# Cross attention and a feed-forward stack on one core: shifting scores in four 64x64 tiles, and the attention residual on ScalarE and GpSimd

## The chip, the core and the metric

The kernel runs on one core of a Trainium2 chip. The core has TensorE (PE; its weight loads are listed as PEld), VectorE (DVE), ScalarE (ACT), GpSimd (POOL), SyncE (SP) for DMA issue, 16 DMA engines, an SBUF and a PSUM of eight banks of 128 partitions by 512 fp32 columns. Each engine has its own list of instructions and runs it in order; lists are coupled by semaphores alone. The metric is device time in microseconds (us) of one execution, the median over runs; less is better.

## What is computed

```python
x = x + xattn(KEY=ctx, VALUE=ctx, QUERY=layernorm(x))
x = x + ffn(layernorm(x))

# xattn: 16 heads of 8; x and ctx are (128, 64, 128) fp32
score = einsum('bhij,bhkj->bhik', k, q) / sqrt(dh)
attn  = softmax(score, axis=1)          # over the HEADS, for each key i and query k
out   = einsum('bhik,bhij->bhjk', attn, v)
res   = out.transpose(0, 2, 1, 3).reshape(B, -1, S).transpose(0, 2, 1) @ Wo.T + bo

# ffn: three blocks; the weights are 4-bit numbers with scales plus a low-rank product
for blk in range(3):
    y = gelu(layernorm(linear(h, 2*blk)))
    h = linear(y, 2*blk + 1) + h
```

The softmax runs over the heads, so the maximum that is subtracted is one number for each (key, query) of a batch entry, over the 16 heads.

## The kernel before

The 8192 tokens are cut into 16 chunks of 512 tokens (8 batch entries). A chunk has four pairs, p = 0 to 3, of two batch entries each; n = 4c + p numbers them. The program has a prologue, then `chunk(c)` for c = 0 to 17 (attention, chunks 2 to 11 in a hardware loop of two chunks a turn, `Fori`), then `step(t)` (feed-forward pipeline, t = 5 to 22, the first five steps being placed inside the last chunks by `EARLY`). Nothing but the written order of each engine's list and the semaphores sets who goes when.

Scores of a pair are a 128 x 1024 fp32 tile in `score_ps[p % 2]`, two banks: the 128 partitions are two batch entries of 64 keys, the columns are 16 heads of 64 queries. A pair goes through this sequence:

- TensorE `scores` (L1041): 16 matmuls of 64x64 weights and 128 columns in fp16, spread over the array's four quadrants (`tile_position`). It waits for `s_exp` of the pair before last, whose buffer it writes.
- VectorE `negmax` (L677): minus the maximum over heads, 128x64, bf16.
- TensorE shift (L1157): two 128x512 matmuls of the identity with `negmax` broadcast over eight heads, added into the two banks; posts `s_shifted`.
- ScalarE `exponentials` (L880): exp of the whole tile into `probs`.
- VectorE `zsum` (L691) and reciprocal `rz` (L694), then GpSimd `probs * rz` (L441), which posts `s_probs`.
- TensorE `att_ps` (L1207): probabilities against block-diagonal values, 16 matmuls of 32 weight columns, each two passes.

In slot p of `chunk(c)` TensorE does scores of pair n+1, the shift of pair n, one piece of the next chunks' preparation (p = 0: transpose of the context L1053; p = 1: `project_q` L1065; p = 2: `project_k` L1071; p = 3: `project_v` L1078), a quarter of `project_out` (L1029, L1013) of two chunks ago, `att_ps` of pair n-2, and at the end the transposed layer-normed input (p = 0, L1059) or the low parts of q (p = 1, L1085) and k (p = 2, L1091). ScalarE copies the results out: `xln_t` (L797), `ctx_tr` (L790), q and k in two fp16 parts each (L804, L810, L818, L824), `att_t` (L902), `v_diag` (L831), `xln` (L782). `project_q` waits for `xln_t`, and `xln_t` for the transposes of L1059. VectorE adds the attention output `wo_ps` to `x_all` (L698), once a chunk at p = 3.

A feed-forward step holds up to three blocks v = 1, 2, 3 of different chunks. On TensorE: the first layers v = 3, 2, 1 (L1231), transposes (L1225, L1284), then the second layer of v = 3 (L1289, into bank 6), of v = 2 and of v = 1 (L1297). On VectorE the step ends with the residual `x_all` of v = 3 (L745), `h` of v = 2 and `h` of v = 1 (L753); the next step's first matmul, the first layer of v = 3, waits for `h` of v = 2.

## Time and profile before

| | |
|---|---|
| three runs | 386.48, 386.40, 384.17 us; median 386.4 |
| the profiled execution | 385.28 us, its span 383.5 us, mean granted clock 0.986 |
| PE, DVE, ACT, POOL busy | 342.6, 327.6, 289.3, 267.3 us |
| attention, steady (66.1 to 167.6 us, chunks 3 to 10) | 12.57 or 12.8 us a chunk |
| feed-forward, steady (315.0 to 345.9 us) | 7.7 us a step |

The span runs from the first to the last record; the rest of the profiled execution's own time, 1.8 us, lies around it. A timeline row gives the start, the duration until the last result, the engine and operation, and in brackets how long the engine had been idle and who ended that. Instructions of ScalarE and VectorE overlap a little, so the next one can start before the printed end; the difference of two starts is what an instruction costs its engine. A row with x16 merges sixteen instructions.

### The profile page before, as it was taken

The numbers are of one execution on the slowest core, as the hardware profiler recorded it, in microseconds if no ns is written. First come the engines' busy times: TensorE is split into PE (matmuls) and PEld (weight loads), VectorE is DVE, ScalarE is ACT, GpSimd is POOL, SyncE is SP. The second block draws the span as 40 slices with busy tenths as digits, with TensorE's granted clock in tenths as the row PEclk, the third lists the DMA queues.
The fourth block names the chain that finished last, engine by engine and source line by source line (L and its number), as shares of the span: only waits on it lengthen the run. The fifth ranks groups of instructions, "written<-read, shape, count | busy, mean of one in ns | idle before, by whom it ended". The sixth has DMA issues, their size and how long they took to land.

```text
span 383.5 us, 12988 instructions
## 1 busy us (share of the span) xinstructions
PE 342.6 (89%) x4772; PEld 251.7 (66%) x4772; DVE 327.6 (85%) x826; ACT 289.3 (75%) x577; POOL 267.3 (70%) x264
## 2 busy tenths in 40 slices
PE   3766899999999999999979777878999999999975
PEld 2343566677667766776656555765888788887854
DVE  6338999999999999999999989668888989978751
ACT  7746887888788878888767436558889989899862
POOL 6322898788877987888797969658777877773311
PEclk9989999999999999999999998999999999999997
DMA  5593775576547754775543200000000010001011
GB/s 162 151 277 107 238 208 163 153 235 196 173 141 228 205 171 150 213 209 180 163 139 112 84 2 2 1 2 2 28 30 28 27 55 27 30 28 56 27 57 55
DMA packets 53122, 43.29 MB, mean 113 GB/s; under 512 B 4496, under 2 KB 46944, under 8 KB 53088
## 3 DMA queue, kind: packets, MB, share of 16 engines
q1 hardware_dynamic: 53088, 42.84, 37.2%
q8 instruction: 21, 0.34, 0.4%
q14 instruction: 13, 0.11, 0.1%
HBM read 26.05 MB, written 16.78 MB: 112 GB/s over the span
## 4 chain that ended last, share of the span: by engine, by line
PE 55%; DVE 26%; issue 9%; POOL 3%; ACT 3%; DMA 2%; POOLq 0%; DVEq 0%; SPq 0%; ACTq 0%
PE score_ps L1231 8%; PE att_ps L1207 6%; DVE zsum L691 6%; DVE negmax L677 6%; PE score_ps L1157 5%; PE wo_ps L1029 5%; DVE st L714 4%; PE score_ps L1041 3%; PE work L1065 3%; PE work L1289 3%; PE work L1071 2%; PE score_ps L1225 2%; PE work L1078 2%; DMA x_all<-in_x 2%; PE score_ps L1297 2%
## 5 line engine op out<-in xcount | busy, mean ns | idle before, releaser
L441 POOL TENSOR_TENSOR probs<-probs,rz 128x1024 f32<-128x1024 f32 x64 | 136.2, 2138 | 38.6 <-DVE rz L694 38.3
L452 POOL TENSOR_TENSOR rs<-ve,minus_half 128x4 f32<-128x4 f32 (+1 forms) x50 | 59.3, 1186 | 49.1 <-DVE ve L630 36.0
L880 ACT ACTIVATE probs<-score_ps 128x1024 f32<-128x1024 f32 x64 | 65.6, 1026 | 21.8 <-PE score_ps L1157 21.4
L677 DVE TENSOR_REDUCE negmax<-score_ps 128x64 bf16<-128x1024 f32 x64 | 75.1, 1174 | 4.1 <-PE score_ps L1041 4.1
L691 DVE TENSOR_REDUCE zsum<-probs 128x64 f32<-128x1024 f32 x64 | 77.3, 1207 | 0.8 <-ACT probs L880 0.8
L1231 PEld LDWEIGHTS score_ps<-lin_t,h 128*128 128x128 f32 x320 | 38.3, 191 | 17.8 <-DVE h L753 16.4
L928 ACT ACTIVATE z<-score_ps,rs 128x128 f32<-128x128 f32 x160 | 45.9, 383 | 2.0 <-POOL rs L452 2.0
L1231 PE MATMUL score_ps<-lin_t,h 128*128 128x128 f32 x320 | 42.9, 281 | 4.7 <-DVE h L753 2.6
L1157 PE MATMUL score_ps<-negmax,ident_bf 128*128 128x512 bf16 x128 | 39.2, 388 | 8.4 <-DVE negmax L677 8.3
L1029 PEld LDWEIGHTS wo_ps<-wo_t,att_t 128*128 128x128 f32 x256 | 37.5, 193 | 13.8 <-issue 12.2
L1207 PE MATMUL att_ps<-probs,v_diag 128*32 128x64 f32 x2048 | 43.9, 225 | 2.3 <-POOL probs L441 2.1
L714 DVE BATCH_NORM_STATS2 st<-score_ps 128x6 f32<-128x128 f32 x160 | 35.6, 285 | 10.7 <-PE score_ps L1231 10.5
L1207 PEld LDWEIGHTS att_ps<-probs,v_diag 128*32 128x32 f32 x2048 | 33.1, 109 | 12.4 <-POOL probs L441 4.8
L1029 PE MATMUL wo_ps<-wo_t,att_t 128*128 128x128 f32 x256 | 39.1, 278 | 0.0
L694 DVE RECIPROCAL rz<-zsum 128x64 f32<-128x64 f32 x64 | 35.4, 553 | 2.2
L1041 PE MATMUL score_ps<-q_stack,k_stack 64*64 64x128 f16 x1024 | 27.0, 223 | 1.2 <-ACT lin_t L773 0.6
L938 ACT ACTIVATE g<-score_ps,cols 128x512 f32<-128x512 f32 x25 | 19.9, 796 | 9.1 <-PE score_ps L1225 9.1
L1041 PEld LDWEIGHTS score_ps<-q_stack,k_stack 64*64 64x64 f16 x1024 | 16.8, 106 | 12.5 <-issue 11.4
L938 ACT ACTIVATE g<-att_ps,cols 128x512 f32<-128x512 f32 x16 | 12.5, 778 | 12.2 <-PE att_ps L1225 12.2
L782 ACT ACTIVATE xln<-x_all,half_rstd 128x128 f32 (+1 forms) x64 | 20.4, 395 | 1.3 <-POOL half_rstd L405 1.3
L831 ACT ACTIVATE v_diag<-work 64x512 f32<-64x512 f32 x32 | 18.8, 587 | 2.8 <-PE work L1078 2.5
L489 DVE BATCH_NORM_STATS2 stats<-x_all 128x6 f32 (+1 forms) x64 | 13.7, 277 | 8.4 <-DMA x_all<-in_x 8.4
(184 smaller groups left out, 671.0 us busy)
## 6 DMA issues: line engine op xcount, KB each, us to landing
q_parts<-parts SPq DMA_DIRECT2D x16, 512.0 KB, 3.5
k_stack<-k_parts SPq DMA_DIRECT2D x32, 256.0 KB, 3.3
q_stack<-q_parts SPq DMA_DIRECT2D x64, 128.0 KB, 2.9
ctx_sb<-in_ctx SPq DMA_DIRECT2D x16, 256.0 KB, 3.7
k_parts<-parts SPq DMA_DIRECT2D x16, 256.0 KB, 2.9
out<-x_all SPq DMA_DIRECT2D x16, 256.0 KB, 2.3
x_all<-in_x SPq DMA_DIRECT2D x14, 256.0 KB, 3.8
x_all<-in_x SPq DMA_DIRECT2D x1, 512.0 KB, 5.0
```

Source lines behind the costliest of these rows:

```text
L441: nc.gpsimd.tensor_tensor(e[:, :, :, :], e[:, :, :, :], by_query.broadcast_to([P, BANDS, SEQ, ADJ]), ALU.mult).then_inc(s_probs, 1)
L452: nc.gpsimd.tensor_tensor(rs2[v][:, lo:hi], ve2[v][:, lo:hi], minus_half[:, lo:hi], ALU.pow).then_inc(p_rs[v], 1)
L677: nc.vector.tensor_reduce(negmax[p % 2][:, :], score_ps[p % 2][:, :].rearrange("p (h k) -> p k h", k=SEQ), AX_X, ALU.max, negate=True).the ...
L691: nc.vector.tensor_reduce(zsum[q][:, :], probs[(p - 1) % 4][:, :, :, :].rearrange("p u k s -> p k u s"), AX_XY, ALU.add).then_inc(s_zsum, 1)
L714: ins = nc.vector.bn_stats(st2[v][:, lo + i, :], src[:, TILE * i:TILE * (i + 1)])
L880: nc.scalar.activation(probs[p][:, :, :, :], score_ps[p % 2][:, :].rearrange("p (u s k) -> p u k s", s=ADJ, k=SEQ), ACT.Exp, scale=SCALE). ...
L928: ins = nc.scalar.activation(z[v][0][:, t, :], src[:, TILE * t:TILE * (t + 1)], ACT.Copy, scale=rs2[v][:, lo + t:lo + t + 1])
L1029: ins = nc.tensor.matmul(wo_ps[:, TILE * t:TILE * (t + 1)], att[:, o, TILE * u:TILE * (u + 1)], wo_t[:, o, b, :], start=False, stop=o == 1 ...
L1041: ins = nc.tensor.matmul(score_ps[mp % 2][SEQ * b:SEQ * (b + 1), c0:c0 + 2 * SEQ], k_stack[mb][half_rows, grp, k0:k0 + SEQ], q_stack[mb][h ...
L1157: ins = nc.tensor.matmul(score_ps[p % 2][:, CHUNK * o:CHUNK * (o + 1)], ident_bf[:, :], negmax[p % 2][:, :].unsqueeze(1).broadcast_to([P, ...
L1207: ins = nc.tensor.matmul(att_ps[32 * grp:32 * (grp + 1), c0:c0 + SEQ], v_diag[mb][:, v0:v0 + 32], probs[mp][:, band(hd), :, hd % ADJ], sta ...
L1231: ins = nc.tensor.matmul(dst[:, TILE * t:TILE * (t + 1)], hk[:, TILE * t:TILE * (t + 1)], lin_t[:, 2 * v - 2, :], start=v == 1 and t == 0, ...
```

## The change

1. The shift (now L1237) is four matmuls of 64x64 weights and 512 columns, one for each quadrant: for the first bank the two diagonal quadrants with `negmax`, for the second the two crossed ones with `negmax_x`, a copy of `negmax` with its halves of 64 partitions exchanged. The copy is two ScalarE instructions a pair (`crossed`, L895, 64x64 bf16). The shift waits for them (`s_crossed`) behind a `nop`, and stands later in TensorE's slot: behind the piece of preparation, and in slot 0 behind the quarter of `project_out` too.
2. For chunks 0 to 13 the attention residual no longer is VectorE's: ScalarE copies `wo_ps` to a new buffer `wo_sb` (L957), and GpSimd adds that to `x_all`.
3. ScalarE's list in a chunk is rewritten: `xln` and `v_diag` are each split in two halves around other work, `xln_t` goes ahead of `ctx_tr`, and the exponentials stand behind one other instruction each.
4. In a feed-forward step the second layer of v = 2 goes ahead of that of v = 3 on TensorE, and `h` of v = 2 ahead of `x_all` on VectorE.

The buffers `negmax_x` (two, 128x64 bf16) and `wo_sb` (128x512 fp32) and the semaphores `s_crossed` and `s_wo_out` are added. The diff's core:

```diff
@@ -235,6 +239,10 @@
+        def by_pool(c):
+            return not isinstance(c, int) or c < NCHUNK - 2
...
@@ -443,6 +451,10 @@
+                    if p == 3 and live(c - 2) and by_pool(c - 2):
+                        pool.wait_ge(s_wo_out, c - 1)
+                        nc.gpsimd.tensor_tensor(x_all[:, c - 2, :, :], wo_sb[:, :].rearrange("p (t d) -> p t d", t=TPC),
+                                                x_all[:, c - 2, :, :], ALU.add).then_inc(s_x2, 1)
...
@@ -692,8 +704,9 @@
-                    if p == 3 and live(c - 2):
+                    if p == 3 and live(c - 2) and not by_pool(c - 2):
+                        dve.wait_ge(s_x2, c - 2)
...
@@ -739,13 +752,12 @@
                 if not isinstance(t, int) or (t >= FIRST_STEP and live(t + 1)):
                     input_stats(t + 1)
 
-                if live(t - 7):
-                    k = t - 7
-                    dve.wait_ge(p_c[3], k + 1)
-                    nc.vector.tensor_tensor(x_all[:, k, :, :], by_token(bank[6]), x_all[:, k, :, :],
-                                            ALU.add).then_inc(p_out, 1)
-                for v, k in ((2, t - 5), (1, t - 3)):
-                    if live(k):
+                for v, k in ((2, t - 5), (3, t - 7), (1, t - 3)):
+                    if v == 3 and live(k):
+                        dve.wait_ge(p_c[3], k + 1)
+                        nc.vector.tensor_tensor(x_all[:, k, :, :], by_token(bank[6]), x_all[:, k, :, :],
+                                                ALU.add).then_inc(p_out, 1)
...
@@ -872,6 +884,17 @@
+                def crossed(p):
+
+                    n = PPC * c + p
+                    act.wait_ge(s_negmax, n + 1)
+                    if some(n - 1):
+                        act.wait_ge(s_shifted, n - 1)
+                    for b in range(2):
+                        src = negmax[p % 2][SEQ * b:SEQ * (b + 1), :]
+                        ins = nc.scalar.activation(negmax_x[p % 2][SEQ * (1 - b):SEQ * (2 - b), :], src, ACT.Copy)
+                    ins.then_inc(s_crossed, 1)
+
@@ -881,42 +904,76 @@
+                def value_block(k, vpar, b):
+
+                    dst = v_diag[vpar][SEQ * b:SEQ * (b + 1), :].rearrange("p (u a e) -> p u a e", a=4, e=16)
+                    return nc.scalar.activation(
+                        dst[:, :, 0:4:3, DH * b:DH * (b + 1)],
+                        work0[SEQ * b:SEQ * (b + 1), :].rearrange("p (u s j) -> p u s j", s=2, j=DH), ACT.Copy)
+
+                def half_of_input(k, lo):
+
+                    for t in (lo, lo + 1):
+                        ins = nc.scalar.activation(xln[:, t, :], x_all[:, k, t, :], ACT.Copy, scale=half_rstd[:, t:t + 1])
+                    return ins
+
+                if live(c):
+                    crossed(0)
+                if live(c + 2) and not (isinstance(c, int) and c == 0):
+                    half_of_input(c + 2, 2).then_inc(s_xln, 1)
                 if live(c):
                     exponentials(0)
                 if live(c + 2):
+                    input_columns(c + 2)
                     context_columns(c + 2, par)
-                    input_columns(c + 2)
                 early_steps(c, 0, step)
+                if live(c):
+                    crossed(1)
+                if live(c + 2):
+                    q_high(c + 2, par)
                 if live(c):
                     exponentials(1)
                 if live(c + 2):
-                    q_high(c + 2, par)
                     q_low(c + 2, par)
-                early_steps(c, 1, step)
-
                 if live(c - 1):
                     act.wait_ge(s_pv, PPC * c)
                     if some(c - 2):
                         act.wait_ge(s_wo, c - 2)
                     nc.scalar.activation(att_t[1 - par][:, :, :].rearrange("p o t -> p (o t)"), att_ps[:, :],
                                          ACT.Copy).then_inc(s_att_t, 1)
+                early_steps(c, 1, step)
+
+                if live(c):
+                    crossed(2)
+                if live(c + 2):
+                    k_high(c + 2, par)
                 if live(c):
                     exponentials(2)
+                if live(c - 2) and by_pool(c - 2):
+                    act.wait_ge(s_wo, c - 1)
+                    if some(c - 2):
+                        act.wait_ge(s_x2, c - 2)
+                    nc.scalar.activation(wo_sb[:, :], wo_ps[:, :], ACT.Copy).then_inc(s_wo_out, 1)
                 if live(c + 2):
-                    k_high(c + 2, par)
                     k_low(c + 2, par)
                 early_steps(c, 2, step)
                 if live(c):
-                    exponentials(3)
-                if live(c + 3):
-                    normalised_input(c + 3)
+                    crossed(3)
                 if live(c + 1):
                     act.wait_ge(s_v_ps, c + 2)
                     if live(c - 1):
                         act.wait_ge(s_pv, PPC * c)
-                    value_blocks(c + 1, 1 - par)
+                    value_block(c + 1, 1 - par, 0)
+                if live(c):
+                    exponentials(3)
+                if live(c + 1):
+                    value_block(c + 1, 1 - par, 1).then_inc(s_v, 1)
+                if live(c + 3):
+                    act.wait_ge(s_rstd, c + 4)
+                    act.wait_ge(s_xln_ps, c + 3)
+                    half_of_input(c + 3, 0)
                 early_steps(c, 3, step)
@@ -1151,20 +1208,15 @@
-                    if live(c):
-                        pe.wait_ge(s_negmax, n + 1)
-                        for o in range(2):
-                            ins = nc.tensor.matmul(score_ps[p % 2][:, CHUNK * o:CHUNK * (o + 1)], ident_bf[:, :],
-                                                   negmax[p % 2][:, :].unsqueeze(1).broadcast_to([P, 8, SEQ]),
-                                                   start=False, stop=True, skip_group_check=True)
-                        ins.then_inc(s_shifted, 1)
-
-                    if isinstance(c, int) and c == 0 and p == 0:
-                        first_layer_rows()
                     if p == 0 and live(c + 2):
                         pe.wait_ge(s_ctxin[par], 16 * (half + 2))
                         pe.wait_ge(s_k_lo, c + 2)
                         transpose_context(par)
+                    if p == 0 and live(c - 2):
+                        ins = project_out(p + 1, att_t[par])
+                        if p == 2:
+                            ins.then_inc(s_wo, 1)
+
                     if p == 1 and live(c + 2):
                         project_q(c + 2)
                     if p == 2 and live(c + 2):
@@ -1176,13 +1228,28 @@
+                    if live(c):
+                        pe.wait_ge(s_crossed, n + 1)
+                        pe.nop(nofuse=True)
+                        for o, maxima in enumerate((negmax[p % 2], negmax_x[p % 2])):
+                            for b in range(2):
+                                r = SEQ * (b ^ o)
+                                ins = nc.tensor.matmul(score_ps[p % 2][SEQ * b:SEQ * (b + 1), CHUNK * o:CHUNK * (o + 1)],
+                                                       ident_bf[r:r + SEQ, r:r + SEQ],
+                                                       maxima[r:r + SEQ, :].unsqueeze(1).broadcast_to([SEQ, 8, SEQ]),
+                                                       start=False, stop=True, skip_group_check=True,
+                                                       tile_position=(r, SEQ * b))
+                        ins.then_inc(s_shifted, 1)
+
+                    if isinstance(c, int) and c == 0 and p == 0:
+                        first_layer_rows()
                     if p == 3 and live(c - 1):
                         pe.wait_ge(s_att_t, c)
                         if some(c - 1):
-                            pe.wait_ge(s_x2, c - 1)
+                            pe.wait_ge(s_wo_out if by_pool(c - 2) else s_x2, c - 1)
                         bias_rows(wo_ps[:, :], 1)
                         project_out(0, att_t[1 - par])
-                    if p < 3 and live(c - 2):
+                    if p in (1, 2) and live(c - 2):
                         ins = project_out(p + 1, att_t[par])
                         if p == 2:
                             ins.then_inc(s_wo, 1)
@@ -1284,18 +1351,20 @@
-                    pe.wait_ge(p_g[3], k + 1)
-                    for i in range(TPC):
-                        ins = nc.tensor.matmul(bank[6][:, TILE * i:TILE * (i + 1)], g[2][:, TILE * i:TILE * (i + 1)],
-                                               lin_t[:, 5, :], start=False, stop=True, skip_group_check=True)
-                    ins.then_inc(p_c[3], 1)
-                for v, k in ((2, t - 5), (1, t - 3)):
+                for v, k in ((2, t - 5), (3, t - 7), (1, t - 3)):
                     if live(k):
                         pe.wait_ge(p_g[v], k + 1)
-                        if some(k):
-                            pe.wait_ge(p_h[v], k)
-                        nc.tensor.matmul(second_layer_bank(v, t), lin_t[:, 2 * v - 1, :], g[v - 1][:, :], start=True,
-                                         stop=True).then_inc(p_c[v], 1)
+                        if v == 3:
+                            for i in range(TPC):
+                                ins = nc.tensor.matmul(bank[6][:, TILE * i:TILE * (i + 1)],
+                                                       g[2][:, TILE * i:TILE * (i + 1)], lin_t[:, 5, :], start=False,
+                                                       stop=True, skip_group_check=True)
+                            ins.then_inc(p_c[3], 1)
+                        else:
+                            if some(k):
+                                pe.wait_ge(p_h[v], k)
+                            nc.tensor.matmul(second_layer_bank(v, t), lin_t[:, 2 * v - 1, :], g[v - 1][:, :],
+                                             start=True, stop=True).then_inc(p_c[v], 1)
```

TensorE in the loop, from the scores in slot 1. `work<-xln_t` is `project_q`, `wo_ps<-` a quarter of `project_out`, `att_ps<-` the product with the values. Before:

```order
L1041 MATMUL score_ps<-q_stack,k_stack 64x128 [waits s_exp]
L1041 MATMUL score_ps<-q_stack,k_stack 64x128 x15
L1155 REGISTER_ALU
L1157 MATMUL score_ps<-negmax,ident_bf 128x512 [waits s_negmax]
L1157 MATMUL score_ps<-negmax,ident_bf 128x512
L1065 MATMUL work<-xln_t,w_t_q 128x512 [waits s_xln_t]
L1029 MATMUL wo_ps<-wo_t,att_t 128x128 x2
L1207 MATMUL att_ps<-probs,v_diag 32x64 [waits s_probs]
L1207 MATMUL att_ps<-probs,v_diag 32x64 x15
L1085 MATMUL work<-parts,neg_ident 128x512 [waits s_q_hi]
```

Now:

```order
L1098 MATMUL score_ps<-q_stack,k_stack 64x128 [waits s_exp]
L1098 MATMUL score_ps<-q_stack,k_stack 64x128 x15
L1122 MATMUL work<-xln_t,w_t_q 128x512 [waits s_xln_t]
L1232 REGISTER_ALU
L1237 MATMUL score_ps<-negmax,ident_bf 64x512 [waits s_crossed]
L1237 MATMUL score_ps<-negmax,ident_bf 64x512
L1237 MATMUL score_ps<-negmax_x,ident_bf 64x512 x2
L1086 MATMUL wo_ps<-wo_t,att_t 128x128 x2
L1274 MATMUL att_ps<-probs,v_diag 32x64 [waits s_probs]
L1274 MATMUL att_ps<-probs,v_diag 32x64 x15
L1142 MATMUL work<-parts,neg_ident 128x512 [waits s_q_hi]
```

The shift stood between the scores and `project_q`; it stands behind `project_q` now, and what it waits for is ScalarE's copy.

ScalarE in the loop, from slot 1 to the start of slot 2. `parts<-work` are the high and low part of q (then of k), `negmax_x` the crossed copies. Before, from the exponentials of pair 1 to those of pair 2:

```order
L879 REGISTER_ALU [waits s_shifted]
L880 ACTIVATE probs<-score_ps 128x1024 [waits s_pv]
L803 REGISTER_ALU [waits s_q_ps]
L804 ACTIVATE parts<-work,cols_h 128x512 [waits s_q_out]
L810 ACTIVATE parts<-work,cols_h 128x512 [waits s_q_rest]
L901 REGISTER_ALU [waits s_pv]
L902 ACTIVATE att_t<-att_ps 128x512 [waits s_wo]
L877 REGISTER_ALU
L879 REGISTER_ALU [waits s_shifted]
L880 ACTIVATE probs<-score_ps 128x1024 [waits s_pv]
```

Now, from the copies for pair 1 to those for pair 2:

```order
L895 ACTIVATE negmax_x<-negmax 64x64 [waits s_shifted,s_negmax]
L895 ACTIVATE negmax_x<-negmax 64x64
L815 REGISTER_ALU [waits s_q_ps]
L816 ACTIVATE parts<-work,cols_h 128x512 [waits s_q_out]
L902 REGISTER_ALU [waits s_shifted]
L903 ACTIVATE probs<-score_ps 128x1024 [waits s_pv]
L822 ACTIVATE parts<-work,cols_h 128x512 [waits s_q_rest]
L942 REGISTER_ALU [waits s_pv]
L943 ACTIVATE att_t<-att_ps 128x512 [waits s_wo]
L890 REGISTER_ALU
L895 ACTIVATE negmax_x<-negmax 64x64 [waits s_shifted,s_negmax]
L895 ACTIVATE negmax_x<-negmax 64x64
```

The copies for pair 2, for which TensorE's shift waits, stand behind the low part of q and `att_t`.

TensorE at the end of a feed-forward step. `work<-lin_t,g` is the second layer of v = 3, `score_ps<-g` that of v = 2, `att_ps<-g` that of v = 1. Before:

```order
L1284 MATMUL work<-ident,h_0 128x128 [waits p_out,p_h2]
L1284 MATMUL work<-ident,h_0 128x128 x3
L1289 MATMUL work<-lin_t,g 128x128 [waits p_g3]
L1289 MATMUL work<-lin_t,g 128x128 x3
L1297 MATMUL score_ps<-g,lin_t 128x512 [waits p_h2,p_g2]
L1297 MATMUL att_ps<-g,lin_t 128x512 [waits p_h1,p_g1]
```

Now:

```order
L1351 MATMUL work<-ident,h_1 128x128 [waits p_out]
L1351 MATMUL work<-ident,h_1 128x128 x3
L1366 MATMUL score_ps<-g,lin_t 128x512 [waits p_h2,p_g2]
L1359 MATMUL work<-lin_t,g 128x128 [waits p_g3]
L1359 MATMUL work<-lin_t,g 128x128 x3
L1366 MATMUL att_ps<-g,lin_t 128x512 [waits p_h1,p_g1]
```

The second layers of v = 2 and v = 3 have changed places.

## Rows read from the trace of the kernel before

**Rows 1.** Page, parts 1 and 4: busy shares, and the chain that ended last.

```profile
PE 342.6 (89%) x4772; PEld 251.7 (66%) x4772; DVE 327.6 (85%) x826; ACT 289.3 (75%) x577; POOL 267.3 (70%) x264
...
PE 55%; DVE 26%; issue 9%; POOL 3%; ACT 3%; DMA 2%; POOLq 0%; DVEq 0%; SPq 0%; ACTq 0%
```

**Rows 2.** Timeline of VectorE, one chunk: start us, us, engine, line, operation, [idle before].

```profile
116.86 1.21 DVE L677 TENSOR_REDUCE negmax<-score_ps 128x64 bf16<-128x1024 f32 x1
...
128.89 0.63 DVE L698 TENSOR_TENSOR x_all<-wo_ps,x_all 128x512 f32 x1
129.43 1.21 DVE L677 TENSOR_REDUCE negmax<-score_ps 128x64 bf16<-128x1024 f32 x1
```

**Rows 3.** Timeline of VectorE, whole span: first maxima of chunks 1 and 2.

```profile
41.60 1.16 DVE L677 TENSOR_REDUCE negmax<-score_ps 128x64 bf16<-128x1024 f32 x1
...
53.51 1.16 DVE L677 TENSOR_REDUCE negmax<-score_ps 128x64 bf16<-128x1024 f32 x1
```

**Rows 4.** Timeline of TensorE, pair slots 0 and 1 of one chunk.

```profile
118.17 0.68 PE L1207 MATMUL att_ps<-probs,v_diag 128*32 128x64 f32 x32
118.77 0.42 PE L1041 MATMUL score_ps<-q_stack,k_stack 64*64 64x128 f16 x16
119.12 0.61 PE L1157 MATMUL score_ps<-negmax,ident_bf 128*128 128x512 bf16 x2
...
121.15 0.66 PE L1059 MATMUL work<-ident,xln 128*128 128x128 f32 x4
121.73 0.42 PE L1041 MATMUL score_ps<-q_stack,k_stack 64*64 64x128 f16 x16
122.08 0.60 PE L1157 MATMUL score_ps<-negmax,ident_bf 128*128 128x512 bf16 x2
122.53 1.09 PE L1065 MATMUL work<-xln_t,w_t_q 128*128 128x512 f32 x2
123.45 0.61 PE L1029 MATMUL wo_ps<-wo_t,att_t 128*128 128x128 f32 x4
...
124.61 0.39 PE L1085 MATMUL work<-parts,neg_ident 128*128 128x512 f16 x1
```

**Rows 5.** Timeline of ScalarE, the same chunk.

```profile
121.84 0.60 ACT L797 ACTIVATE xln_t<-work 128x512 f32<-128x512 f32 x1 [0.48 <-PE work L1059]
122.80 1.02 ACT L880 ACTIVATE probs<-score_ps 128x1024 f32<-128x1024 f32 x1 [0.37 <-PE score_ps L1157]
...
125.04 0.69 ACT L810 ACTIVATE parts<-work,cols_h 128x512 f16<-128x512 f32 x1 [0.62 <-PE work L1085]
```

**Rows 6.** Timeline of ScalarE, prologue: two 16-column copies.

```profile
8.99 0.17 ACT L847 ACTIVATE cols<-score_ps 128x16 f32<-128x16 f32 x1
9.06 0.18 ACT L848 ACTIVATE cols_h<-score_ps 128x16 f32<-128x16 f32 x1
```

**Rows 7.** Groups by line and form: count, busy us, mean ns, idle before.

```profile
L782 ACT ACTIVATE xln<-x_all,half_rstd 128x128 f32 x40 | 12.7, 392 | 0.0
...
L476 POOL TENSOR_TENSOR z<-z,nmr 128x512 f32<-128x512 f32 x16 | 16.6, 1039 | 2.3
```

**Rows 8.** Timeline of GpSimd, the same chunk as 2, 4 and 5.

```profile
123.42 2.14 POOL L441 TENSOR_TENSOR probs<-probs,rz 128x1024 f32<-128x1024 f32 x1 [1.42 <-DVE rz L694]
```

**Rows 9.** Timeline of TensorE, feed-forward steps.

```profile
313.72 1.02 PE L1297 MATMUL att_ps<-g,lin_t 128*128 128x512 f32 x2
314.95 1.16 PE L1231 MATMUL score_ps<-lin_t,h 128*128 128x128 f32 x8 [0.20 <-DVE h L753]
...
321.67 1.02 PE L1297 MATMUL att_ps<-g,lin_t 128*128 128x512 f32 x2
322.67 1.16 PE L1231 MATMUL score_ps<-lin_t,h 128*128 128x128 f32 x8
...
365.63 1.16 PE L1231 MATMUL score_ps<-lin_t,h 128*128 128x128 f32 x8 [0.84 <-DVE h L753]
```

**Rows 10.** Timeline of all engines, feed-forward step: the VectorE row between.

```profile
313.56 0.67 DVE L745 TENSOR_TENSOR x_all<-work,x_all 128x512 f32 x1
```

5 lines of the change are left out of this document (added).

## The prediction

> **What bounds the kernel now.** I read the page first: TensorE is busy 89% of the span and VectorE 85%, ScalarE 75%, GpSimd 70%, and the chain that ended last runs 55% over TensorE and 26% over VectorE [rows 1]. With two engines that near to each other the shares say little, so I went to the timeline of one attention chunk. VectorE's list from one chunk's first maximum to the next takes 12.57 us, from 116.86 to 129.43, and no row in between shows a wait [rows 2]; its last piece is the residual, 0.54 us by the two starts 128.89 and 129.43. Chunk 1, which has no residual yet, took 11.91 us [rows 3]: that is VectorE's floor without it. TensorE in the same chunk shows no wait either: `project_q` starts at 122.53, 0.09 after `xln_t` has its last result (121.84 + 0.60), and that is just when the shift in front of it is through (122.08 + 0.43) [rows 4, 5]. So **both engines are full at the same 12.6 us**. Every second chunk takes 12.8, by the loop's branch, and the ten chunks 2 to 11 average 12.67. An edit that relieves VectorE alone buys nothing there; what TensorE's list gains or loses decides.
>
> In the feed-forward steps the second layer of v = 1 starts at 321.67 and takes TensorE 0.86 us; the next step's first matmul starts at 322.67, 0.14 us late, and at 314.95 it is 0.37 late (313.72 + 0.86 = 314.58), waiting for VectorE's `h` [rows 9]. VectorE had put `x_all` of v = 3 ahead of that `h`, at 313.56, 0.67 long [rows 10]. In the draining steps the same wait is 0.84 us once [rows 9].
>
> **The change, part by part.** All sums are against the profiled execution, 385.28 us (383.5 of span and 1.8 around it). The median of the three runs is 386.4, so I add 1.1 to compare with it.
>
> *The shift.* Two full matmuls of 512 columns took 0.45 us between starts (122.08 to 122.53, and 0.43 of it is columns, 0.22 each) [rows 4]. Now four of 512 columns stand on four quadrants. That quadrants overlap the scores show: 16 matmuls of 128 columns would be 4 x 0.22 = 0.88 us one after another, and take 0.35 (118.77 to 119.12) [rows 4], about 0.02 each to issue. Four at once should so take 0.22 + 3 x 0.02 = 0.28. But entering small tiles from full ones has a price: the four input transposes (0.11 each, 0.44) and the scores behind them start 0.58 apart (121.15 to 121.73), a gap of 0.14; from `att_ps` to the scores, small to small, there is none (118.17 to 118.77 is the 0.60 of 32 matmuls), and from scores to the full shift there is none [rows 4]. The old shift followed the scores without a gap; the new one follows full matmuls. So slots 1 to 3 change by -0.45 + 0.28 + 0.14 = -0.03 each, and slot 0, where `att_ps` now follows the shift directly and saves such a gap, by some -0.1: **-0.2 us a chunk**.
>
> The Trainium skill says in TensorEngine Tiling (Array Packing), Key Properties, that a change of the tiling mode drains TensorE, which speaks against this shift. The trace agrees at the entry (0.14) and not at the exit (0); by the page's rule, counted on both sides, the shift would cost another 4 x 0.14 us a chunk.
>
> *The order around it.* From the first input transpose to `project_q` there are 1.38 us (121.15 to 122.53): 0.69 until ScalarE starts `xln_t`, 0.60 for it, 0.09 until TensorE goes on [rows 4, 5]. TensorE filled that with transposes, scores and shift. Now the shift stands behind `project_q`, and only transposes and scores are left: they end 0.93 us in (121.15 to 122.08). **TensorE waits 0.45 us** there in each chunk; ScalarE cannot be sooner, as it starts `xln_t` on the transposes' end already today.
>
> *The crossed copies.* Two ScalarE instructions of 64 columns for each pair, 128 in all. The nearest rows: 16-column copies take 0.17 to 0.18 us and start 0.07 apart [rows 6]; the 128-column `xln` takes 0.39 with a scale from SBUF [rows 7]. I take 0.22 each and 0.11 between starts, nearer to the first since no scale is read: the pair is ready 0.33 us after it begins. Ends: 0.25 and 0.68. The Trainium skill (ScalarE: Activation LUTs, What ACT_TABLE_LOAD costs) gives 186 ns + 0.833 ns a column less 93 ns of overlap: 0.24 and 0.15, so 0.39 for the pair; no row here has this shape. That page's price would add about half a microsecond to the total.
>
> When is the pair ready? For slot 2, from `project_q` at 0: it is through at 0.92 (122.53 to 123.45), the shift at 1.06 to 1.34, `project_out` and `att_ps` 1.16 more (123.45 to 124.61) [rows 4], so the low product of q starts at 2.5. ScalarE takes its result 0.43 later (124.61 to 125.04) [rows 4, 5], at 2.93, then copies `att_t` (0.5 each), and begins the pair at 4.0: ready 4.33. TensorE meanwhile did the low product, scores (0.1 and 0.35) and `project_k` (0.9) and would start the shift at 4.2. **It waits about 0.2 us.** In slots 0, 1 and 3 the same count leaves the pair ready 0 to 0.4 us early. The exponentials stay hidden: the shift's end to exp was 0.29 (122.08 + 0.43 to 122.80 [rows 4, 5]), and the instruction put ahead of each fills it.
>
> ScalarE's own load, some 10.3 us a chunk (12.57 less its 2.2 of waits), grows by 8 x 0.11 and the 0.5 of `wo_sb` to 11.7: below 12.6, so no bound. Sum for the ten full chunks: 10 x (-0.2 + 0.45 + 0.2) = **+4.5 us**. In chunks 0 and 1 TensorE has no `project_out` in most slots and VectorE rules: 0.
>
> *The residual.* VectorE loses 14 x 0.54 us. In the ten full chunks it costs and gives nothing, as TensorE sets the pace; its cover is TensorE's list. In chunks 12 to 15 TensorE is lighter and VectorE sets it: at most 4 x 0.54 = 2.2, at least 0 (TensorE waits longer for the copies there); I take **-1.5**. GpSimd gets 14 additions of 1.04 us, the price of a 128x512 with two inputs [rows 7], and had idle times of up to 1.42 before a pair's product [rows 8]; queued behind the addition is the product of the chunk's last pair, which `att_ps` needs two slots later. Cover: that slack of over 1 us. The wait of `project_out` for `wo_sb` lies a slot behind the copy: 0.
>
> *Feed-forward order.* `h` of v = 2 comes up to 0.89 us sooner on TensorE (the eight matmuls of L1289) and 0.67 on VectorE, more than the lateness of 0.14 to 0.37 a step [rows 9, 10]. What is late next is TensorE itself. `x_all` of v = 3 moves 0.9 back; only the store behind it waits, and in the next step the transposes into the bank it frees, 5 us later. Over the thirteen steps from 260 to 360 us the late starts add to 3.6 us, less 0.2 for each turn of the loop that remain; the drain adds 0.84 once. Of 4.5 I take **-3.5**, with ends 0 and -5.
>
> **Sum:** 385.3 + 4.5 - 1.5 - 3.5 = 384.8 us, or **385.9** beside the median. Two gains and a loss that cancel.
>
> **Rivals.**
> (a) *The likeliest, as summed*: 385.9, with its own range of 382 to 390. Chance 0.38.
> (b) *Faster: entering small tiles is hidden.* If the wait for the copies lets TensorE load the first weights ahead, the gap of 0.14 isn't paid four times: -0.56 a chunk, -5.6 in all, 380.3. For it: the weight loads have a queue of their own, idle a third of the span [rows 1]. Against: the scores' gap is there though their wait was over long before [rows 4]. Chance 0.30, with fuller gains in the feed-forward part as a second way there.
> (c) *Slower: the copies lead.* If a pair takes 0.68 us (the `xln` price [rows 7]) in place of 0.33, TensorE waits 0.35 more in slots 2 and 0 and some 0.15 in the others together: 0.85 a chunk, 394.4. It decides from about 0.5 us a pair. For it: ScalarE's list is in order, and copies stand behind results that TensorE has yet to make. Against: two shorter copies took 0.25 together [rows 6]. Chance 0.16.
> (d) *Leaving small tiles costs as much as entering*: 4 x 0.14 a chunk, 385.9 + 5.6 = 391.5. That is the page's drain in full. Against: scores to shift show nothing [rows 4]. Chance 0.08.
> (e) *The change doesn't do what it says*: the quadrants run one after another with 512 columns, 0.88 + 0.14 for a shift, +0.6 us each, 64 times: +38, 424. Against: the scores' 0.35. Chance 0.03. The remaining 0.05 lies beyond either end, most of it above.
>
> **Numbers.** A difference of under 1% (3.9 us) can't be told from none here. Faster by over 1% (below 382.5): most of (b) and a tenth of (a), 0.32. Slower (above 390.3): (c), (d), (e) and the rest, 0.30. Same: 0.38. The range takes (b) with its spread and just reaches (c): 378 to 394.
>
> **What would show it.** In the changed profile: four shift matmuls starting within 0.1 us and the next instruction 0.3 after the first (else e); a gap of 0.1 to 0.15 before them with the copies done (else b); a wait of 0.4 to 0.5 of `project_q` for `xln_t` (else the order was harmless); the copies at 0.2 to 0.25 us each (else c); full chunks at 13.1 us, VectorE with half a microsecond of idle time or more in each; feed-forward steps at 7.5 with no wait before the first layer of v = 3. I am wrong if full chunks run below 12.6, which only a TensorE list without the two waits allows, or if the steps stay at 7.7, which would put another chain than `h` behind them.

## The result, and the profile after

The changed kernel takes **412.25 us** (median of four runs, 408.06 to 412.85) against 385.71 us for the kernel before on the same chip (four runs, 384.17 to 386.48): ratio 1.068, interval 1.063 to 1.073. The forecast was 385.9 with a range to 394; it called no change likeliest, and the result lies well above. The profiled execution took 412.33 us, its span is 410.4 us.

Page of the changed kernel, parts 1 and 4 (compare [rows 1]): busy time with share of the span and instructions, and the chain that ended last by engine.

```profile
PE 354.3 (86%) x4900; PEld 253.1 (62%) x4900; DVE 327.6 (80%) x812; ACT 332.0 (81%) x719; POOL 285.4 (70%) x278
...
PE 50%; ACT 18%; issue 14%; DVE 12%; DMA 2%; POOL 2%; SPq 1%; ACTq 1%; POOLq 0%; DVEq 0%
```

ScalarE's share of the chain went from 3% to 18%. VectorE's busy time is the same 327.6 us as before, in a longer span and with 14 instructions fewer (the residuals that it no longer adds).

Page, part 5, the lines of the shift, of the sum over heads and of the copies: count, busy us, mean ns, idle before.

```profile
L703 DVE TENSOR_REDUCE zsum<-probs 128x64 f32<-128x1024 f32 x64 | 77.9, 1218 | 32.5 <-ACT probs L903 32.5
...
L1237 PE MATMUL score_ps<-negmax,ident_bf 64*64 64x512 bf16 x128 | 27.1, 410 | 24.4 <-ACT negmax_x L895 24.2
...
L895 ACT ACTIVATE negmax_x<-negmax 64x64 bf16<-64x64 bf16 x128 | 32.5, 254 | 8.5 <-DVE negmax L689 6.5
```

TensorE waits 24 us for the copies and VectorE 32 us for the exponentials behind them; before, VectorE had waited 0.8 us there in all. Timeline of ScalarE, slots 1 and 2 of a chunk (compare [rows 5]):

```profile
132.62 0.60 ACT L809 ACTIVATE xln_t<-work 128x512 f32<-128x512 f32 x1
133.11 0.59 ACT L802 ACTIVATE ctx_tr<-work 128x512 f32<-128x512 f32 x1
133.73 0.52 ACT L895 ACTIVATE negmax_x<-negmax 64x64 bf16<-64x64 bf16 x2
...
137.00 0.59 ACT L943 ACTIVATE att_t<-att_ps 128x512 f32<-128x512 f32 x1
137.62 0.52 ACT L895 ACTIVATE negmax_x<-negmax 64x64 bf16<-64x64 bf16 x2
138.16 0.69 ACT L830 ACTIVATE parts<-work,cols_h 128x512 f16<-128x512 f32 x1
```

Other neighbours overlap: `ctx_tr` starts 0.49 after `xln_t`, which takes 0.60. A pair of copies overlaps with nothing. It starts 0.62 after `ctx_tr` (whose 0.59 are over), lasts 0.52, and the next instruction starts 0.54 after it (138.16 - 137.62). So a pair costs ScalarE 0.54 us and also takes away the overlap of some 0.12 that the instruction ahead had with its follower, four times a chunk.

Timeline of TensorE, slots 0 to 2 of the same chunk (compare [rows 4]):

```profile
130.98 0.40 PE L1237 MATMUL score_ps<-negmax,ident_bf 64*64 64x512 bf16 x2 [0.41 <-ACT negmax_x L895]
130.98 0.40 PE L1237 MATMUL score_ps<-negmax_x,ident_bf 64*64 64x512 bf16 x2
131.32 0.68 PE L1274 MATMUL att_ps<-probs,v_diag 128*32 128x64 f32 x32
...
133.27 1.13 PE L1122 MATMUL work<-xln_t,w_t_q 128*128 128x512 f32 x2
...
138.28 0.40 PE L1237 MATMUL score_ps<-negmax,ident_bf 64*64 64x512 bf16 x2 [0.50 <-ACT negmax_x L895]
...
138.62 0.71 PE L1086 MATMUL wo_ps<-wo_t,att_t 128*128 128x128 f32 x4
```

The four quadrants do run at once: the next instruction starts 0.34 us after them. They wait for the copies 0.41 and 0.50 us in slots 0 and 2.

Where the 26.9 us of span went, by the first maxima of chunks 2, 12 and 15 (53.51, 180.18, 221.67 before; 55.45, 199.10, 247.34 after) and the start of the last `h` (e1 is the first experiment below):

| stretch | before | after | difference | e1 (full shift) - before |
|---|---|---|---|---|
| to chunk 2 | 53.51 | 55.45 | +1.9 | +0.8 |
| chunks 2 to 11 | 126.67 | 143.65 | +17.0 | +6.8 |
| chunks 12 to 14 | 41.49 | 48.24 | +6.8 | +3.7 |
| chunk 15 to the last `h` | 148.48 | 150.67 | +2.2 | -4.1 |
| rest | 13.35 | 12.39 | -1.0 | -0.9 |

### The profile page after: what moved, and what is told of

The parts are those of the page before. It is cut to its first block, busy times and chain, and to the rows that moved or that the text cites. A ratio compares the mean times of both kernels' runs of the same rounds, so it can differ in the third digit from the quotient of the medians.

```text
span 410.4 us, 13533 instructions
## 1 busy us (share of the span) xinstructions
PE 354.3 (86%) x4900; PEld 253.1 (62%) x4900; DVE 327.6 (80%) x812; ACT 332.0 (81%) x719; POOL 285.4 (70%) x278
## 4 chain that ended last, share of the span: by engine, by line
PE 50%; ACT 18%; issue 14%; DVE 12%; DMA 2%; POOL 2%; SPq 1%; ACTq 1%; POOLq 0%; DVEq 0%
PE score_ps L1298 9%; PE wo_ps L1086 5%; PE att_ps L1274 5%; ACT probs L903 4%; PE work L1122 4%; ACT negmax_x L895 4%; PE score_ps L1237 3%; PE work L1359 3%; PE score_ps L1366 3%; DVE zsum L703 3%; DVE negmax L689 3%; PE att_ps L1366 3%; PE score_ps L1292 2%; ACT xln L917 2%; ACT att_t L943 2%
## 5 line engine op out<-in xcount | busy, mean ns | idle before, releaser
L1237 PE MATMUL score_ps<-negmax,ident_bf 64*64 64x512 bf16 x128 | 27.1, 410 | 24.4 <-ACT negmax_x L895 24.2
L1274 PE MATMUL att_ps<-probs,v_diag 128*32 128x64 f32 x2048 | 45.2, 229 | 1.3 <-POOL probs L449 1.2
L1086 PE MATMUL wo_ps<-wo_t,att_t 128*128 128x128 f32 x256 | 45.7, 308 | 0.0
L1298 PE MATMUL score_ps<-lin_t,h 128*128 128x128 f32 x320 | 41.9, 277 | 2.1 <-DVE x_all L711 0.9
L1274 PEld LDWEIGHTS att_ps<-probs,v_diag 128*32 128x32 f32 x2048 | 34.2, 112 | 11.7 <-issue 4.5
L1237 PEld LDWEIGHTS score_ps<-negmax,ident_bf 64*64 64x64 bf16 x128 | 8.3, 105 | 53.0 <-issue 51.1
L895 ACT ACTIVATE negmax_x<-negmax 64x64 bf16<-64x64 bf16 x128 | 32.5, 254 | 8.5 <-DVE negmax L689 6.5
L1098 PE MATMUL score_ps<-q_stack,k_stack 64*64 64x128 f16 x1024 | 28.3, 231 | 4.6 <-ACT probs L903 3.9
L1098 PEld LDWEIGHTS score_ps<-q_stack,k_stack 64*64 64x64 f16 x1024 | 18.4, 111 | 17.3 <-issue 16.3
L1237 PE MATMUL score_ps<-negmax_x,ident_bf 64*64 64x512 bf16 x128 | 27.1, 420 | 0.0
L910 ACT ACTIVATE v_diag<-work 64x512 f32<-64x512 f32 x30 | 17.7, 591 | 7.5 <-PE work L1135 7.2
```

Source lines behind the costliest of these rows:

```text
L895: ins = nc.scalar.activation(negmax_x[p % 2][SEQ * (1 - b):SEQ * (2 - b), :], src, ACT.Copy)
L1086: ins = nc.tensor.matmul(wo_ps[:, TILE * t:TILE * (t + 1)], att[:, o, TILE * u:TILE * (u + 1)], wo_t[:, o, b, :], start=False, stop=o == 1 ...
L1098: ins = nc.tensor.matmul(score_ps[mp % 2][SEQ * b:SEQ * (b + 1), c0:c0 + 2 * SEQ], k_stack[mb][half_rows, grp, k0:k0 + SEQ], q_stack[mb][h ...
L1237: ins = nc.tensor.matmul(score_ps[p % 2][SEQ * b:SEQ * (b + 1), CHUNK * o:CHUNK * (o + 1)], ident_bf[r:r + SEQ, r:r + SEQ], maxima[r:r + S ...
L1274: ins = nc.tensor.matmul(att_ps[32 * grp:32 * (grp + 1), c0:c0 + SEQ], v_diag[mb][:, v0:v0 + 32], probs[mp][:, band(hd), :, hd % ADJ], sta ...
L1298: ins = nc.tensor.matmul(dst[:, TILE * t:TILE * (t + 1)], hk[:, TILE * t:TILE * (t + 1)], lin_t[:, 2 * v - 2, :], start=v == 1 and t == 0, ...
```

## Experiments

Lines of code that are only moved are not shown. Ratios are against the kernel before on the same chip.

### e1: all but the quadrants and the copies

```diff
-                    crossed(0)
...
-                        pe.wait_ge(s_crossed, n + 1)
-                        pe.nop(nofuse=True)
-                        for o, maxima in enumerate((negmax[p % 2], negmax_x[p % 2])):
...
+                        pe.wait_ge(s_negmax, n + 1)
+                        for o in range(2):
+                            ins = nc.tensor.matmul(score_ps[p % 2][:, CHUNK * o:CHUNK * (o + 1)], ident_bf[:, :],
+                                                   negmax[p % 2][:, :].unsqueeze(1).broadcast_to([P, 8, SEQ]),
+                                                   start=False, stop=True, skip_group_check=True)
```

> The changed kernel with the shift as two full 128x512 matmuls again, at its new place in the list, and without the crossed copies; new orders and the residual on ScalarE and GpSimd stay. Theory 'copies' (each crossed copy costs ScalarE 0.27 us with no overlap, which makes ScalarE the bound at 14.4 us a chunk): a full chunk falls to the 13.1 us that the wait of project_q for xln_t leaves, and most of the loss goes: 388 to 393 us. Rival 'orders' (the new lists themselves couple the engines badly): chunks stay above 13.8 us and the time above 400.

Measured: 392.04 us (four runs, 391.60 to 392.86), ratio 1.022 (1.015 to 1.029). A full chunk (mean of chunks 3 to 11) takes 13.35 us, against 14.40 changed and 12.67 before. So about **20 of the 27 us come with the copies and the quadrants**, and 6 to 8 with the rest. TensorE's timeline of this kernel shows where most of a chunk's share of that rest lies (the full shift stands at the changed kernel's place in TensorE's list):

```profile
138.53 0.66 PE L1108 MATMUL work<-ident,xln 128*128 128x128 f32 x4
139.28 0.42 PE L1090 MATMUL score_ps<-q_stack,k_stack 64*64 64x128 f16 x16
139.88 1.13 PE L1114 MATMUL work<-xln_t,w_t_q 128*128 128x512 f32 x2 [0.17 <-ACT xln_t L809]
140.84 0.59 PE L1226 MATMUL score_ps<-negmax,ident_bf 128*128 128x512 bf16 x2
141.27 0.61 PE L1078 MATMUL wo_ps<-wo_t,att_t 128*128 128x128 f32 x4
141.81 0.68 PE L1261 MATMUL att_ps<-probs,v_diag 128*32 128x64 f32 x32
```

The scores stand 0.75 behind the transposes (0.58 before) and `project_q` 0.60 behind the scores (they need 0.35): 0.42 us of waits in this place, where the prediction had 0.45. The new orders together cost some 0.7 a chunk (13.35 less 12.67).

### e2 and e3: the feed-forward order alone, the residual alone

e2 is the kernel before with part 4 of the change, e3 with part 2.

> The kernel before with the feed-forward order alone changed (second layer and h of v = 2 first). If the 0.26 us a step and the shorter drain seen between the two traces are this edit's: 380 to 382 us (4 to 5 less), steps at 7.47 us. Rival: the steps got faster because they started from another state after the attention, then 385 to 386 and 7.7 us.

> The kernel before with the attention residual alone moved: ScalarE copies wo_ps between the high and low part of k, GpSimd adds. Theory 'copies': ScalarE has room for 0.6 us, TensorE sets the pace, full chunks stay at 12.6 to 12.7 and the last chunks gain up to 1.5 us: 384 to 386. Rival 'residual' (the ScalarE copy and the GpSimd addition delay the exponentials and products): chunks above 12.9, 389 or more.

Measured: e2 382.27 us (ten runs, 380.67 to 383.66), ratio 0.996 (0.993 to 0.999). e3 386.17 us (ten runs, 382.57 to 388.19), ratio 1.004 (1.000 to 1.009). The feed-forward order gains, though less by the medians (1.8 us) than by the profiled spans (4.6 us, 3.5 of it between chunk 15 and the last `h`). The residual, forecast at -1.5, gains nothing that the runs can tell (the interval begins at 1.000), and the profiled execution, one of e3's slowest, lost 3.0 us in chunks 12 to 14, where the gain was to be. Timeline of VectorE and of GpSimd in e3 there:

```profile
192.76 1.90 DVE L649 SCALAR_TENSOR_TENSOR ag<-st 128x4 f32<-128x4 f32 x1
194.58 0.15 DVE L651 TENSOR_TENSOR ag<-st 128x4 f32<-128x4 f32 x1
194.66 1.23 DVE L652 TENSOR_TENSOR ag<-st 128x4 f32<-128x4 f32 x1
```

```profile
190.41 4.23 POOL L447 TENSOR_TENSOR probs<-probs,rz 128x1024 f32<-128x1024 f32 x2
194.60 1.26 POOL L454 TENSOR_TENSOR x_all<-wo_sb,x_all 128x512 f32<-128x512 f32 x1
```

Two VectorE instructions of four columns take 1.90 and 1.23 us. The first ends with GpSimd's product (190.41 + 4.23 = 194.64), as in the kernel before; the second with the new addition (195.86 and 195.89), while their neighbour L651 takes 0.15. The Trainium skill says in SBUF — State Buffer, Who interferes with whom, that a VectorE instruction with two SBUF inputs contends with a GpSimd instruction that reads SBUF, and that their shared port pair is an exclusive lock. The trace agrees: 1.23 against 0.15, and an end together with GpSimd's.

### e4: quadrants and copies in the old order

The kernel before with `crossed(p)` right ahead of `exponentials(p)`, and the four matmuls right behind the scores.

> The kernel before with the four-quadrant shift alone: it stands right behind the scores as the old shift did, and ScalarE makes the two crossed copies right ahead of each exponential; list orders and residual as before. Theory 'copies': ScalarE needs 10.4 us of old work and 8 x 0.27 and lost overlap, some 13.1 us a chunk, and TensorE waits at the shift for the copies with everything behind it: 13.2 to 14.5 us a chunk, 394 to 410 us. Rival 'orders': the copies are hidden in ScalarE's old waits, chunks at 12.5 to 12.8, 384 to 388 us.

Measured: 452.86 us (four runs, 452.42 to 454.67), ratio 1.179 (1.172 to 1.187), a full chunk 17.4 us. Far above what was expected. Timelines of TensorE and of ScalarE:

```profile
147.49 0.40 PE L1177 MATMUL score_ps<-negmax,ident_bf 64*64 64x512 bf16 x2 [1.55 <-ACT negmax_x L885]
```

```profile
146.82 0.52 ACT L885 ACTIVATE negmax_x<-negmax 64x64 bf16<-64x64 bf16 x2
147.94 1.02 ACT L893 ACTIVATE probs<-score_ps 128x1024 f32<-128x1024 f32 x1 [0.60 <-PE score_ps L1177]
```

Both engines wait for each other in every slot: TensorE 1.05 to 1.55 us for the copies, ScalarE 0.6 to 0.7 for the shift. So the new orders, dear as they are (0.7 a chunk in e1), save about 40 us once the quadrant shift is there: 412 instead of 453.

### e5 and e6: one or two copies on all 128 partitions

The copies don't exchange the halves here, so the second bank is shifted by the wrong maxima; times are read, not values.

```diff
-                    for b in range(2):
-                        src = negmax[p % 2][SEQ * b:SEQ * (b + 1), :]
-                        ins = nc.scalar.activation(negmax_x[p % 2][SEQ * (1 - b):SEQ * (2 - b), :], src, ACT.Copy)
-                    ins.then_inc(s_crossed, 1)
+                    nc.scalar.activation(negmax_x[p % 2][:, :], negmax[p % 2][:, :], ACT.Copy).then_inc(s_crossed, 1)
```

That is e5. e6 has two such copies, the second into columns of its own in a wider `negmax_x`:

```diff
+                    for b in range(2):
+                        ins = nc.scalar.activation(negmax_x[p % 2][:, SEQ * b:SEQ * (b + 1)], negmax[p % 2][:, :], ACT.Copy)
+                    ins.then_inc(s_crossed, 1)
```

> The changed kernel with ONE ScalarE copy of 128x64 in place of the two crossed 64x64 ones (the halves are not exchanged, so the second bank's scores are shifted by the other batch entry's maxima). Theory 'copies bind ScalarE by instruction': four instructions of 0.27 us less a chunk and, if a full-height copy overlaps its neighbours as others do, the overlap back: full chunks at 13.3 to 13.6 us, 392 to 398 us. Rival 'latency' (the extra hop through ScalarE costs, not its time): chunks stay above 14.1, 408 or more.

> The changed kernel with two ScalarE copies of 128x64 each, same count and columns as the crossed ones, but on all 128 partitions (halves not exchanged, so half of the heads are shifted by other maxima). If half-height instructions are what doesn't overlap (v_diag at 64 partitions didn't either, 0.59 us from start to start): the copies start 0.1 to 0.15 us apart and the chunk falls to 13.4 to 13.7 us, 394 to 399 us. Rival: small bf16 copies take 0.26 us whatever their height: 14.3 us a chunk, 410 us, as the changed kernel.

Measured: e5 398.73 us (two runs, 398.45 and 399.01), ratio 1.037 (1.029 to 1.045), a chunk 13.55. e6 402.88 us (402.00 and 403.75), ratio 1.048 (1.039 to 1.056), a chunk 13.84. Both lie above the times expected, but the fall from 14.40 is there. Timeline of ScalarE in e6:

```profile
134.00 0.59 ACT L942 ACTIVATE att_t<-att_ps 128x512 f32<-128x512 f32 x1
134.47 0.40 ACT L894 ACTIVATE negmax_x<-negmax 128x64 bf16<-128x64 bf16 x2
134.84 0.69 ACT L830 ACTIVATE parts<-work,cols_h 128x512 f16<-128x512 f32 x1
```

Two copies of twice the partitions take 0.40 instead of 0.52, and overlap with both neighbours (0.47 after `att_t`, 0.37 to the next). The crossed 64x64 copies cost 0.56 us a chunk more than these. In e5, with one copy, the profile lists no wait of TensorE for it between 66 and 180 us, and a chunk still takes 0.20 us more than with the full shift (13.55 against 13.35).

### e7: the copies on VectorE

```diff
-                        ins = nc.scalar.activation(negmax_x[p % 2][SEQ * (1 - b):SEQ * (2 - b), :], src, ACT.Copy)
...
+                        dve.wait_ge(s_negmax, n + 1)
...
+                            ins = nc.vector.tensor_copy(negmax_x[p % 2][SEQ * (1 - b):SEQ * (2 - b), :], src)
```

> The changed kernel with the two crossed copies made by VectorE right behind negmax. Theory 'ScalarE is the bound': ScalarE falls back to 11.7 us of work, VectorE rises to 12.0 plus 8 x 0.1 to 0.2, so full chunks run at 13.3 to 13.8 us, the total 392 to 400. Rival 'quadrant shift or orders': still above 14.2, 408 or more.

Measured: 477.28 us (four runs, 476.76 to 477.68), ratio 1.241 (1.234 to 1.248), the slowest of all. Timelines of VectorE and GpSimd:

```profile
139.63 2.15 DVE L695 COPY negmax_x<-negmax 64x64 bf16<-64x64 bf16 x2
```

```profile
138.40 2.13 POOL L449 TENSOR_TENSOR probs<-probs,rz 128x1024 f32<-128x1024 f32 x1 [2.14 <-DVE rz L711]
140.48 1.26 POOL L456 TENSOR_TENSOR x_all<-wo_sb,x_all 128x512 f32 x1
```

A copy takes 0.17 us at best (the shortest of the 128) and 0.71 on average; this pair ends when GpSimd's addition does (141.78 and 141.74). The expectation looked at VectorE's free time and not at what it shares with GpSimd. The Trainium skill's SBUF — State Buffer, Who interferes with whom, has it that a VectorE instruction in a two-port mode and a GpSimd instruction block each other; the ends agree, the mode itself no run shows.

### e8 and e9: GpSimd's addition behind the feed-forward step

e8 is e3 with the addition written behind the early step of its slot; e9 is that with part 4 of the change.

```diff
+                    early_steps(c, p, step)
                     if p == 3 and live(c - 2) and by_pool(c - 2):
                         pool.wait_ge(s_wo_out, c - 1)
                         nc.gpsimd.tensor_tensor(x_all[:, c - 2, :, :], wo_sb[:, :].rearrange("p (t d) -> p t d", t=TPC),
                                                 x_all[:, c - 2, :, :], ALU.add).then_inc(s_x2, 1)
-                    early_steps(c, p, step)
```

> The kernel before with only the residual on ScalarE and GpSimd, and GpSimd's addition written behind the feed-forward step that is placed in the same slot, instead of ahead of it. With the addition ahead, chunks 12 to 14 took 44.5 us from maximum to maximum (before: 41.5), a small VectorE instruction with two inputs from SBUF taking 1.23 us in place of 0.15 beside the addition. Theory 'port': the loss is that and GpSimd's delay of the step; behind the step chunks 12 to 14 take about 42.0 us and the total is 382.5 to 385.0. Rival 'ScalarE': the copy of the attention output delays the step's ScalarE work; then chunks 12 to 14 stay at 44 to 45 and the total at 386.

> The kernel before with the feed-forward order and the residual on ScalarE and GpSimd, GpSimd's addition standing behind the early feed-forward step in its list. Theory 'port': in the run with the residual alone VectorE's small two-input operations stood still until GpSimd's addition ended (1.23 us in place of 0.15, in chunks 12 and 13); with the addition behind the step they don't meet it, and what the last chunks lost comes back: 377 to 380 us. Rival (the last chunks lose by ScalarE's copy or the later x_all): no better than 381 to 383.

Measured: **e9 380.05 us** (four runs, 379.94 to 381.33), ratio 0.989 (0.983 to 0.995), the fastest version here, 1.1% below the kernel before. e8 384.42 us (ten runs, 383.32 to 387.00), ratio 0.997 (0.995 to 1.000). VectorE in e9, the second of these instructions:

```profile
194.92 0.15 DVE L652 TENSOR_TENSOR ag<-st 128x4 f32<-128x4 f32 x1
```

1.23 has become 0.15. Chunks 12 to 14 take 41.9 us in e9, the 42.0 that the 'port' theory had for e8; e9's total lies at the upper end of the 377 to 380 expected. In e8's profiled execution (its slowest run) they took 43.8, neither the expected 42.0 nor e3's 44.5; L652 is back at 0.15 there too, but the granted clock was 0.78 in a stretch of them that ran at 1.00 in e9:

```profile
210.00:224.00 14.00, 10.73 (x220) 7.62 (x219) 12.81 (x19) 5.81 (x8) 11.60 (x10) 0.78 0.27 80
```

(the last three numbers are clock, DMA share and GB/s). So the port accounts for about 1.1 us in each of two chunks, and the rest of e3's loss is not settled.

### e10: the full shift from chunk 12 on

```diff
+                    if live(c) and isinstance(c, int) and c >= 12:
+                        pe.wait_ge(s_negmax, n + 1)
+                        for o in range(2):
+                            ins = nc.tensor.matmul(score_ps[p % 2][:, CHUNK * o:CHUNK * (o + 1)], ident_bf[:, :],
...
-                    if live(c):
+                    elif live(c):
                         pe.wait_ge(s_crossed, n + 1)
...
-                if live(c):
+                if live(c) and not (isinstance(c, int) and c >= 12):
                     crossed(0)
```

> The changed kernel, but chunks 12 to 15 shift with the two full matmuls of before, straight from the maxima and without the ScalarE copies (at the changed kernel's place in TensorE's list). The changed kernel lost 3.0 us against the full shift everywhere in chunks 12 to 14 and 6.3 us from chunk 15's first maximum to the end of the feed-forward steps; TensorE's granted clock was lower there too (0.68 and 0.70 in two stretches of 16 us, against 0.79 once). Theory 'copies': both losses come from the copies of the last chunks, the lower clock with them, since TensorE waits more; then chunks 12 to 14 take about 45.2 us and the rest after them 144.4, total 402 to 405. Rival 'history': the tail is slow by what went before (the throttle's state after 11 slow chunks); then chunks 12 to 14 gain at most 3 us, the stretch behind them stays near 150, total 408 to 411.

Measured: 403.48 us (four runs, 402.61 to 404.51), ratio 1.046 (1.042 to 1.050). Chunks 12 to 14 take 44.3 us, and 144.2 pass from chunk 15's first maximum to the last `h`; with the copies it is 48.2 and 150.7, with e1 45.2 and 144.4. The copies and quadrants of the last four chunks cost 8.8 us by the medians and 9.6 by the profiled spans, nearly as much as those of the ten full ones (143.65 - 133.45 = 10.2 us against e1). TensorE waits 12.0 us for the copies between 199 and 262 us in the changed kernel, and 6.8 us for the maxima between 199 and 256 in e10. Here the feed-forward's early steps stand in the same ScalarE list, ahead of copies: for one of them, `z` at 257.34, ScalarE waits 2.36 us for GpSimd, with a pair of copies behind it (258.50). Windows of the changed kernel and of e10 (us, then busy PE, PEld, DVE, ACT, POOL, then the granted clock):

```profile
240.00:252.00 12.00, 11.12 (x186) 8.10 (x182) 8.93 (x11) 6.86 (x13) 8.35 (x5) 0.67 0.01 3
```

```profile
240.00:252.00 12.00, 9.27 (x183) 7.15 (x181) 11.23 (x24) 5.55 (x11) 10.05 (x7) 0.94 0.01 3
```

0.67 is a mean over stretches at 2.4 and at 1.2 GHz; 240 to 246 us ran at 0.50 throughout, that is 1.2 GHz, and in the 6 us before TensorE had been busy for 2.63. The two windows are the same microseconds, not quite the same work; at the same distance from chunk 15's first maximum (235.75 to 247.75) e10's clock is 0.95. The clock comes back with the copies gone, with the slow chunks ahead unchanged. So the low clock goes with the waits of this stretch, and not with what lay before. About 5 of the nearly 10 us are longer waits (12.0 against 6.8); how much of the rest is the clock, and how much of the waits the clock made, stays open.

### e11 and e12: is it the crossing or the height?

e11 (first diff) copies each half to its own half; e12 (second) copies the lower half twice. Neither exchanges the maxima, so here too times are read and not values.

```diff
-                        ins = nc.scalar.activation(negmax_x[p % 2][SEQ * (1 - b):SEQ * (2 - b), :], src, ACT.Copy)
+                        ins = nc.scalar.activation(negmax_x[p % 2][SEQ * b:SEQ * (b + 1), :], src, ACT.Copy)
```

```diff
-                        src = negmax[p % 2][SEQ * b:SEQ * (b + 1), :]
-                        ins = nc.scalar.activation(negmax_x[p % 2][SEQ * (1 - b):SEQ * (2 - b), :], src, ACT.Copy)
+                        src = negmax[p % 2][0:SEQ, :]
+                        ins = nc.scalar.activation(negmax_x[p % 2][0:SEQ, SEQ * b:SEQ * (b + 1)], src, ACT.Copy)
```

> The changed kernel with each 64x64 copy going to the same half of the partitions that it reads, instead of the other (the maxima of the two batch entries are so not exchanged, and the second bank is shifted by the wrong ones). Theory 'half height': an instruction on 64 of 128 partitions does not overlap with its neighbours, whatever the halves; the pair stays at 0.52 us and a full chunk at 14.4 us, total 407 to 413. Rival 'crossing': it is the exchange of halves that costs; then the pair falls to 0.39 to 0.40 us as with 128 partitions, a chunk to 13.8 and the total to 401 to 404.

> The changed kernel with both 64x64 copies of a pair reading and writing partitions 0 to 63 (the second into columns of its own that nobody reads); the quadrants with rows 64 to 127 take the maxima straight from negmax. So the second bank is shifted by unexchanged maxima. With 64-partition copies that stayed in their own half, a full chunk took 14.05 us, the first copy (partitions 0 to 63) beginning 0.12 to 0.14 before the end of the 128-partition instruction ahead, the second (64 to 127) not before the end of the first. Theory 'first partition': two ScalarE instructions overlap when both read and both write from the same first partition, however many they cover. Then the pair takes 0.38 to 0.40 us and the next instruction overlaps too, a full chunk takes 13.7 to 13.9 us as with 128 partitions, and the total is 400 to 404. Rival 'half height': a 64-partition instruction cannot overlap with the 64-partition one behind it; the pair stays at 0.51, a chunk at 14.0 to 14.1, the total at 405 to 408.

Measured: e11 406.31 us (one run), a chunk 14.05; neither theory, as it lies between them. e12 402.47 us (one run), a chunk 13.83, the 'first partition' theory's number and e6's. ScalarE in e11, then in e12:

```profile
129.59 0.59 ACT L802 ACTIVATE ctx_tr<-work 128x512 f32<-128x512 f32 x1
130.07 0.51 ACT L895 ACTIVATE negmax_x<-negmax 64x64 bf16<-64x64 bf16 x2
...
133.88 0.51 ACT L895 ACTIVATE negmax_x<-negmax 64x64 bf16<-64x64 bf16 x2
134.41 0.69 ACT L830 ACTIVATE parts<-work,cols_h 128x512 f16<-128x512 f32 x1
```

```profile
133.63 0.59 ACT L943 ACTIVATE att_t<-att_ps 128x512 f32<-128x512 f32 x1
134.11 0.39 ACT L895 ACTIVATE negmax_x<-negmax 64x64 bf16<-64x64 bf16 x2
134.48 0.69 ACT L830 ACTIVATE parts<-work,cols_h 128x512 f16<-128x512 f32 x1
```

In e11 the copy from partitions 0 to 63 overlaps with the instruction ahead (0.48 between starts); the copy from 64 does not overlap with it, nor the next one with that (0.53). In e12 everything overlaps, at 64 partitions as at 128. So **not the height but the first partition decides**: neighbours on ScalarE overlap in these rows when both begin at partition 0, and don't when one of them reads or writes from 64. No row has two neighbours that both begin at 64. The crossed copies have one side at 0 and the other at 64, and overlap with nothing either: in these rows one side at 64 is enough.

TensorE in e12, slot 1, isolates the other half of the change, since the shift waits for nothing here:

```profile
129.97 1.13 PE L1122 MATMUL work<-xln_t,w_t_q 128*128 128x512 f32 x2 [0.17 <-ACT xln_t L809]
131.03 0.41 PE L1237 MATMUL score_ps<-negmax,ident_bf 64*64 64x512 bf16 x3
...
131.37 0.71 PE L1086 MATMUL wo_ps<-wo_t,att_t 128*128 128x128 f32 x4
132.01 0.67 PE L1274 MATMUL att_ps<-probs,v_diag 128*32 128x64 f32 x32
```

From `project_q` to `att_ps` it is 2.04 us (129.97 to 132.01); with the full shift, in e1, 1.93 (139.88 to 141.81). The shift itself fell from 0.43 to 0.34, but `project_q` ahead of it grew from 0.96 to 1.06 and the four `wo_ps` behind it from 0.54 to 0.64. Even with nothing to wait for, **four quadrants cost TensorE 0.1 us more than the full shift** in this slot.

## Why the prediction was wrong

*What bounds the kernel* was read rightly: both engines full, TensorE's list decides, and e3's full chunks, with VectorE's residual gone, stay at 12.67.

*The crossed copies* are the step that failed, and in two ways. First, the price of 0.33 a pair, with copies 0.11 apart, rested on the two 16-column copies [rows 6], which both begin at partition 0. Measured were 0.54 and 0.12 of lost overlap. The kernel before had a row that shows such a loss, and the prediction didn't look for it:

```profile
118.60 1.18 ACT L831 ACTIVATE v_diag<-work 64x512 f32<-64x512 f32 x2
119.84 1.03 ACT L880 ACTIVATE probs<-score_ps 128x1024 f32<-128x1024 f32 x1
```

Two half copies, the second at partition 64, and nothing overlaps: 2 x 0.59, and the exponentials 1.24 behind their start. Second, ScalarE's load was put at 11.7, "below 12.6, so no bound". It was 13.19 us in a chunk of 14.42, and by the rows the engines wait for each other in a ring: TensorE's shift for the copies, the exponentials for the shift, the next copies for the exponentials ahead of them in ScalarE's list. In the prediction's own count for slot 2, from `project_q` at 0 (133.27), the pair was to begin at 4.0 and to be ready at 4.33; it began at 4.35 (137.62) and was ready at 4.87, and TensorE waited 0.50 in place of 0.2. (That count gives the low product 0.1, where the kernel before has 0.32 to the scores behind it; its 4.2 comes out only with the 0.32.)

It is rival (c) that happened, at 0.54 past its point of decision of 0.5 a pair. It had 0.16 of the chance, and its 394.4 left out that VectorE too waits behind the copies (the exponentials come later; 16.4 us between 66 and 180) and that the last four chunks suffer most.

TensorE's list over a full chunk, 14.40 against 12.67, adds up to about that: 0.7 for the order (e1), 0.2 for the quadrants (e5 against e1, 13.55 and 13.35, with no listed wait for a copy), and TensorE's waits for the copies. The latter are shown by the changed kernel and by e12 from 66 to 180 us, as us in total, times, longest:

```profile
PE score_ps L1237 <- ACT negmax_x L895: 6.9, 16, 0.5
```

```profile
PE score_ps L1237 <- ACT negmax_x L895: 2.4, 12, 0.2
```

6.9 over eight chunks is 0.86 each (with 0.2 predicted for one slot and none for the others), and e12, at nearly the predicted price, has 0.30. That difference of 0.56 is all of e12's gain (14.40 to 13.83). 0.7 + 0.2 + 0.86 = 1.76, measured 1.73.

*The shift itself*: 0.34 for 0.28 predicted, the entry 0.10 (`project_q` 1.06 instead of 0.96) for 0.14 predicted. The exit, forecast at 0, costs 0.10 where full fp32 matmuls follow (slots 1 and 2), and nothing to speak of before the bias row of slot 3. In slot 0 `att_ps`, itself small tiles, follows and pays no entry of its own, as predicted. So rival (d) was half right, in two slots. Rival (b) fell at the entry, rival (e) at the 0.34. The Trainium skill says in TensorEngine Tiling (Array Packing), Key Properties, that a change of the tiling mode drains TensorE. The trace of e12 agrees on both sides in slot 1, with 0.10 each.

*The order around it*: 0.45 predicted for `project_q`, 0.42 measured (e1). The other 0.3 of e1's chunk were not forecast. With ScalarE's new list the exponentials come later (9.6 us of VectorE's waits in e1 from 66 to 180 us, 0.8 before); that this is the 0.3 no run shows.

*The residual*: -1.5 forecast; e3's median lies 2.1 above the kernel before, which is not clear of no change. "It costs and gives nothing" held for the full chunks. In the last chunks GpSimd's addition holds VectorE's small instruction, and GpSimd's slack, which the prediction did check, was not the question; with the addition behind the step (e8, e9) no loss is clear of noise.

*Feed-forward order*: right in its mechanism. The steps take 7.47 us instead of 7.73 (the seven from 321.06 on; 7.58 between the two shown), and no first layer of v = 3 waits in the steady part, as TensorE in the changed kernel shows (compare [rows 9]):

```profile
313.48 1.02 PE L1366 MATMUL att_ps<-g,lin_t 128*128 128x512 f32 x2
314.34 1.16 PE L1298 MATMUL score_ps<-lin_t,h 128*128 128x128 f32 x8
...
321.06 1.02 PE L1366 MATMUL att_ps<-g,lin_t 128*128 128x512 f32 x2
321.92 1.05 PE L1298 MATMUL score_ps<-lin_t,h 128*128 128x128 f32 x8
```

Each starts 0.86 behind the second layer, TensorE's own pace. -3.5 was taken; e2 has -1.8 by its median and -4.6 by its profiled execution, its fastest.

*Chunks 0, 1 and 12 to 15* were costed at 0 and -1.5. The first gave +1.9, the last with the stretch behind them +8.9 (6.75 + 2.19), although the feed-forward order gains there: the copies and quadrants cost nearly as much in the four last chunks (e10) as in ten full ones. The prediction summed their cost only over the steady chunks.

## What to carry to other kernels

Before moving small work to an engine "with room", find a row of the same shape, the same first partition and the same neighbours. Take the time from start to start, not the busy time, and then ask who stands behind it in that list. Where two engines hand a tile to and fro (shift, exponentials, next shift), a step added on one is paid by both, whatever the shares say. And a move to GpSimd is to be checked against the small two-input instructions of VectorE at its side, not only against GpSimd's own slack.

## What the runs showed of the hardware

- ScalarE instructions overlap with their neighbours by about 0.12 us when both begin at partition 0 and neither has to wait, and not when one reads or writes from partition 64: copies 0.54 a pair when crossed, 0.37 when both begin at 0 (e12), 0.37 at full height (e6). Two neighbours that both begin at 64 were not tried. The Trainium skill's ScalarE: Activation LUTs, What ACT_TABLE_LOAD costs, gives back-to-back instructions an overlap of about 93 ns; the crossed copies show none, those that begin at 0 some 0.12, while its price for the single one (0.24 us) is near the 0.25 measured.
- Four 64x64 quadrants at 512 columns run in 0.34 us together, but 0.10 is lost ahead of them and 0.10 behind, between full fp32 matmuls (e12): 0.54 in all, against 0.43 for the two full ones (e1).
- A bf16 copy of 64x64 on VectorE takes from 0.17 to over 1 us, 0.71 on average, in a kernel where GpSimd works beside it (e7).
- A VectorE instruction of four columns with two inputs from SBUF takes 1.23 us beside a GpSimd addition and 0.15 without (e3, e9).
